# Attention denominators: inverses taken one key-tile pair earlier, spread by two transfers of 64 rows instead of one of 128

## The reference, cut to what matters

```python
scores = jnp.einsum('bhsr,bhlr->bhsl', q_r, k_r)       # 16 heads, 100 rows, 1444 keys
attn = jax.nn.softmax(scores, axis=-1)
ctx_c = jnp.einsum('bhsl,bld->bhsd', attn, kv_r)       # 64 values per head and row
ctx_lat = jnp.einsum('bhsd,hkd->bhsk', ctx_c, w_kc_kv)
return ctx @ Wo.T
```

## Time and profile before

| what | value |
|---|---|
| runs | 3496.22, 3482.72, 4833.27 us; median 3496.22 |
| profiled execution | 3511.37 us, span 3509.6 us |
| mean granted TensorE clock in it | 0.911 |
| latent attention (groups and heads) | about 964.8 to 3255 us of the span |
| one group in steady state | 290.5 us (1265.2 to 1555.7 us) |
| busy in that group: PE, DVE, POOL, ACT | 256.66, 213.18, 169.33, 137.54 us |

### The profile page before, as it was taken

One profiled execution on the slowest core, in us unless ns is written; L12 is line 12 of the kernel. 1 busy time (PEld: TensorE's weight loads), 2 busy tenths in 40 slices (PEclk: granted clock), 3 DMA queues, 4 the chain that ended last, 5 costly groups with the idle time before them and its releaser, 6 DMA issues. The chain is left out here.

```text
span 3509.6 us, 61563 instructions
## 1 busy us (share of the span) xinstructions
PE 2942.7 (84%) x18344; PEld 1971.0 (56%) x18352; DVE 2449.7 (70%) x4170; ACT 1488.0 (42%) x3074; POOL 1640.1 (47%) x1196
## 2 busy tenths in 40 slices
PE   6999979999788998998898898889889889887244
PEld 4777779998544554554454455555446455444123
DVE  5877754444576786687677677668777767775787
ACT  1323322222254454445435435444443553544456
POOL 0000022222465565555556565556565656564567
PEclk9888879999899998999999999899999999998566
DMA  4000010002101000100101000110010100010100
GB/s 105 0 0 0 0 50 5 9 9 51 29 13 19 20 13 15 22 13 15 19 14 21 14 20 16 16 21 16 14 21 11 19 16 16 10 45 13 60 13 24
DMA packets 128325, 71.04 MB, mean 20 GB/s; under 512 B 81663, under 2 KB 122591, under 8 KB 127961
## 3 DMA queue, kind: packets, MB, share of 16 engines
q1 hardware_dynamic: 128024, 67.44, 8.6%
HBM read 56.95 MB, written 10.04 MB: 19 GB/s over the span
## 5 line engine op out<-in xcount | busy, mean ns | idle before, releaser
L1178 POOL TENSOR_TENSOR c_psum<-c_p 120x800 f32<-120x800 f32 (+1 forms) x384 | 745.5, 1945 | 737.0 <-ACT c_p L1462 339.9
L1462 ACT ACTIVATE c_p<-c_s_ps 120x400 f32<-120x400 f32 (+1 forms) x1536 | 659.2, 507 | 497.0 <-PE c_s_ps L1623 439.6
L1256 DVE TENSOR_REDUCE c_mpart<-c_m_ps 128x1 f32<-128x484 f32 x1080 | 656.5, 651 | 164.5 <-PE c_m_ps L1530 159.9
L1635 PE MATMUL c_o_ps<-c_p,c_val 120*64 120x400 f32 (+1 forms) x3072 | 629.2, 533 | 27.5 <-ACT c_onum L1429 16.3
L1530 PE MATMUL c_m_ps<-c_kmax,c_q 64*128 64x484 f32 x1080 | 340.8, 471 | 174.1 <-DVE c_mpart L1256 170.3
L1530 PEld LDWEIGHTS c_m_ps<-c_kmax,c_q 64*128 64x128 f32 x1080 | 153.2, 194 | 405.8 <-DVE c_mpart L1256 329.4
L1283 DVE TENSOR_TENSOR c_acc<-c_acc,c_psum 120x800 f32<-120x800 f32 x256 | 322.4, 1259 | 63.8 <-POOL c_psum L1178 61.8
L1635 PEld LDWEIGHTS c_o_ps<-c_p,c_val 120*64 120x64 f32 (+1 forms) x3072 | 194.4, 141 | 292.4 <-issue 170.1
L1169 POOL TENSOR_TENSOR l_rr<-c_psum,l_rr 96x400 f32<-96x400 f32 x256 | 260.8, 1039 | 208.0 <-DVE l_rr L1305 207.9
L1566 PE MATMUL c_s_ps<-c_xt,l_a 128*96 128x400 f32 x1536 | 309.6, 352 | 23.4 <-DVE l_rr L1305 21.5
L1619 PE MATMUL c_s_ps<-c_q,c_k 64*120 64x400 f32 (+1 forms) x1536 | 319.8, 375 | 2.3 <-ACT c_p L1462 2.3
(11 more groups left out here) (251 smaller groups left out, 5075.3 us busy)
## 6 DMA issues: line engine op xcount, KB each, us to landing
c_rdb<-l_denominators SPq DMA_DIRECT2D x64, 200.0 KB
c_kv<-in_ctx SPq DMA_DIRECT2D x32, 360.0 KB
c_mrow<-c_mneg SPq DMA_DIRECT2D x288, 0.5 KB, 2.0
x_rows<-in_x SPq DMA_DIRECT2D x4, 800.0 KB
x_spill<-x_rows SPq DMA_DIRECT2D x8, 400.0 KB
l_xa<-x_spill SPq DMA_DIRECT2D x8, 400.0 KB
c_xr<-x_spill SPq DMA_DIRECT2D x32, 100.0 KB
x_spill<-c_xr SPq DMA_DIRECT2D x32, 100.0 KB
```

The source lines that it names most:

```text
L1178: g.tensor_tensor(psum[0:k, u % 2, :], p[0:k, 2 * u % 4, :], p[0:k, (2 * u + 1) % 4, :], ALU.add).then_inc(psum_ready, 1)
L1256: v.tensor_reduce(mpart[:, t, bank:bank + 1], m_ps[:, bank, 0:4 * KP], AX.X, ALU.max, negate=True).then_inc(mpart_ready, 1)
L1462: a.activation(p[0:k, w % 4, i * HALFQ:(i + 1) * HALFQ], s_ps[0:k, (2 * w + i) % 4, 0:HALFQ], ACT.Exp).then_inc(exp_ready, 1)
L1635: mm = pe.matmul(o_ps[i * DL:(i + 1) * DL, 0:HALFQ], val[0:k, j % 2, r, :], p[0:k, w % 4, i * HALFQ:(i + 1) * HALFQ], start=(r == 0), stop ...
```

## The change

Three edits, all in `phase_l1_attention`. DVE's `invert` stands after pair q = 2 instead of q = 3 (slots 5 and 17 instead of 7 and 19). The spread is two transfers of 64 partitions each, which count 32 on the semaphore together. In SP's list the write of the inverses goes ahead of `load_combined(it, j, 6)` (first half) or of `load_combined(it, j + 1, 2)` (second half), and the spread goes ahead of `load_combined(it, j + 1, 3)`. In the heads the order stays, and only the two transfers are new. The fold stays where it was, behind `load_combined(it, j, 5)` or `(it, j + 1, 1)`.

```diff
@@ spread_inverses
                     sp.wait_ge(ct_ready, PRIMED + ch)
-                    sp.dma_start(rdb[:], io["den"].rearrange("(i n) -> i n", i=2).unsqueeze(1).broadcast_to((2, DL, HALFQ))).then_inc(rdb_loaded, 16)
+                    for i in range(2):
+                        sp.dma_start(rdb[i * DL:(i + 1) * DL, :], io["den"][i * HALFQ:(i + 1) * HALFQ].partition_broadcast(DL)).then_inc(rdb_loaded, 16)
@@ SP, group, first half
                         if j > 0:
                             fold_denominators(b * CH - 1)
+                        if j > 0:
+                            write_inverses(b * CH - 1)
                         load_combined(it, j, 6)
                         if j > 0:
-                            write_inverses(b * CH - 1)
                             spread_inverses(b * CH - 1)
@@ SP, group, second half
                             load_combined(it, j + 1, 0)
                             load_combined(it, j + 1, 1)
                         fold_denominators(b * CH)
+                        write_inverses(b * CH)
                         if j + 1 < G:
                             load_combined(it, j + 1, 2)
+                        spread_inverses(b * CH)
+                        if j + 1 < G:
                             load_combined(it, j + 1, 3)
-                        write_inverses(b * CH)
-                        spread_inverses(b * CH)
@@ DVE, normalise
-                    v.wait_ge(rdb_loaded, 16 * (ch + 1))
+                    v.wait_ge(rdb_loaded, 32 * (ch + 1))
@@ DVE, group
-                        if (j, c) != (0, 0) and q == 3:
+                        if (j, c) != (0, 0) and q == 2:
                             invert(ch - 1)
```

## The result

The changed kernel takes 3389.89 us (median of 4 runs, 3388.19 to 3399.07); the kernel before took 3499.6 us beside it. Ratio 0.9707, 95% interval 0.9666 to 0.9749: faster by 2.9%. In a second series it had 3402.29 us and 0.9753 (0.9708 to 0.9799). The profiled execution took 3399.07 us against 3511.37, so 112.3 us less, where 75 were forecast. The ratio compares fast runs alone, so the run of 4833.27 us of the kernel before is not in it. Faster by over 2% had been given 0.46, within 2% 0.51.

A forecast was written before the change was run, and what follows sets the result against it. Bound by PE and DVE waiting for each other, with 153.3 us of DVE waits for the spread: (17.2 - 8.3) x 8 = 71 plus 4 gives 75 us off 3511.4, 3436, or 3421 on the median's scale; range 3375 to 3475.

The forecast's parts named there:

- What bounds the kernel, and the narrow transfer: DVE waits 153.3 us for the spread inverses, whose transfer runs on about two of 16 DMA engines, 7.3 us to use.
- All waits at the normalising go: At DVE's L1268, all 18.2 us of waiting per group for the spread inverses would go.
- What that is worth: Gain from the removed waits at L1268: 17.2 us per group, bounds 9.3 and 22.
- The first, second and fourth place: Three of a group's eight waits at L1268, with PE standing still behind: on the path, 13.6 us with the slow clock.
- The other five: The group's remaining waits at L1268, without a PE gap behind: 8.0 us of DVE's time, worth 3.6.
- The inverse two slots earlier: New DVE waits for the fold at L1264, 6.6 us per group; with one slow stretch of clock a loss of 8.3.
- The one more slow stretch: Behind the new waits at L1264, PE's clock at its lower level once more per group, costing 1.7 us.
- The end: The last L1268 waits 5.65 us; the shorter landing takes 4.7 off, 0.7 already counted: 4 us gained.
- the waits are traded: Rival: DVE's time returns only where PE stands still, against 8.3 us new per group; 26 us gained, 3470; chance 0.29.
- the slower case: Rival: the fold wait at L1264 costs more than the spread wait it replaces; 15 us slower, 3511; chance 0.07.
- The case of more coming back: Rival: new waits fall into DVE's later ones, clock stays 1.00: 134 us gained, 3363, in part 3390; chance 0.11.

The follow-up runs named there:

- the inverse back: The changed kernel with DVE's inverse moved back behind pair q = 3, all else as changed: 3356.57 us, ratio 0.9615; a second time 3349.53 us, 0.9596.
- the fold ahead: The changed kernel with the fold issued ahead of load_combined(it, 1, 5) and of load_combined(it, j + 1, 1) for j = 0 and 1: 3366.27 us, ratio 0.9626.
- The dose: The changed kernel with the inverse behind q = 3, plus an unread 128x128 DVE copy ahead of each of a group's 40 accumulator additions: 3420.04 us, ratio 0.9797.
- the kernel with both edits: The changed kernel with the inverse behind q = 3 and the fold ahead of the row transfers: 3347.56 us, ratio 0.9586; a second time 3341.19 us, 0.9562.

## Why the prediction was right, and where its sizes were off

*What bounds the kernel, and the narrow transfer:* right, and now shown. With the order of before, 64 rows outermost take the wait from 153.3 to 18.6 us; in the changed order two transfers of the old shape leave 39.0 us, where one leaves 37.2. From the first issue to the use 2.6 us were taken; it is 3.4. It did no harm in the groups, where the spread had time to spare.

*All waits at the normalising go:* right, 1.8 us are left, at the end.

*What that is worth, 17.2 us per group:* 18.7 with the inverse back, where 0.6 us of waiting is left. The sum hid two errors of opposite sign, and that it came out so near is luck. The first, second and fourth place were put at 13.6 us. Made wide alone they give 290.1 - 281.2 = 8.9 us, and with the wait that this leaves in the first place (273.3 - 271.4) 10.8. I had added 4.0 us of clock on top of PE's gaps; which part of the 13.6 was too large the runs don't say. The other five were put at 3.6 of 8.0 us, because PE shows no gap behind them; they gave 7.9 for the 9.3 us of waiting that went per group, so some 7 for 8.0. The step that failed was to read "no gap of PE behind the wait" as "not on the path". DVE's next longer pause does not take the wait up: it comes 5.1 us after the fifth place and lasts 2.2 us, in all of the six groups, both in the kernel before and in the one with the two wide transfers alone.

*The inverse two slots earlier:* the three places and their waits came out as worked (3.8, 1.75 and 1.6 forecast; 3.79, 0.99 and 1.62 measured; some 57 us forecast, 51.7 measured). Their price was put at 8.3 us per group and measured at 5.7. The one more slow stretch did come, 3.4 us at the lower level behind PE's gap of 3.42 us in every group; it was put at half of 3.4. What was too high is the sum of the two terms, 6.6 of waiting and 1.7 of clock: taking the waits away by the fold ahead gave back only 4.0 us per group. Moving the inverse back after that gave 2.3 to 2.6 more, without any wait, and for this the prediction had no term. In the kernel with the fold ahead the clock is at its lower level for 12.5 us per group instead of 5.7, so the 4.0 us are net of that; why the slow stretches moved so stays open. This item is the larger part of the error, 2.6 of 4.1 us per group; the other 1.5 is in the item before.

*The end:* 4 us forecast, 3.9 measured, in part by luck. The wait was to fall by 4.7 us, of which 0.7 had been counted with the groups; it fell by 3.9, because the pair takes 3.4 us to use and not 2.6.

*The rivals:* that the waits are traded is refuted, as is the slower case. The case of more coming back (3363 to 3390, chance 0.11) is where the time landed, at its edge. Both of its reasons held in part. Most slow stretches went with PE's gaps, though the clock did not stay at 1.00 behind the new waits. And these cost less than their length, 4.0 us for 6.5 by the fold ahead, where this case had 3.

From the kernel before (158.1 us of waits, 290.1 us per group) to the one with the inverse back (6.5 us, 271.4) it is 18.7 us for 19.0 of waiting. The dose shows 0.72 per us for DVE's time, and single steps lie between 0.6 (the fold ahead) and 1.2 (the first, second and fourth place, 8.9 us for 7.5). The clock rose with it from 0.95 to 0.98, and PE's busy time fell from 1527.12 to 1482.98 us in six groups for the same matmuls. I varied neither by itself, so what share is theirs is not shown. The clock alone does not order the kernels: the changed one has the higher clock, 0.99, and is slower by 5.7 us per group than the one with the inverse back at 0.98.

## What to carry to other kernels

Before a wait for a transfer is hidden by moving things, look at how wide the transfer runs: here the one with 2 outermost kept the DMA engines 11% busy for 5.7 us, and the same bytes with 64 outermost kept them 29% busy for under 2. When a step is moved earlier, ask for its inputs too; here the fold that feeds it stayed behind other transfers in one queue, and a third of the gain (5.7 of 18.7 us per group) was given back with this move. And a wait on the second-busiest engine can cost most of its length, here 0.8 us per us, also where the busiest engine shows no gap right behind it: look whether the waiting engine's later pauses can take it up.

## What the runs showed of the hardware

The kernel with the fold ahead has no waits at either place and still takes 273.1 us per group, 2.3 and 2.6 more than the two runs with the inverse back as well (270.8 and 270.5). DVE is busy 1302.95 us in six groups there and 1295.35 in the better kernel, with the same instructions. The difference lies in an operation with two SBUF inputs, `c_k<-c_kd,c_k`: its 72 instructions are busy 71.4 us against 60.6. The third batch of one group, in the kernel with the fold ahead, DVE's and POOL's timelines:

```profile
1950.31 2.31 DVE L1255 TENSOR_TENSOR c_k<-c_kd,c_k 64x484 fp32r<-64x484 f32 x1
...
1950.22 1.88 POOL L1187 TENSOR_TENSOR c_psum<-c_p 120x800 f32<-120x800 f32 x1 [1.83 <-ACT c_p L1471]
```

and in the kernel with both edits:

```profile
1946.32 0.64 DVE L1255 TENSOR_TENSOR c_k<-c_kd,c_k 64x484 fp32r<-64x484 f32 x1
...
1946.34 2.38 POOL L1187 TENSOR_TENSOR c_psum<-c_p 120x800 f32<-120x800 f32 x1 [1.93 <-ACT c_p L1471]
```

Where POOL is 0.09 us ahead, DVE's operation takes 2.31 us, until 0.5 us after POOL's end; where DVE is 0.02 us ahead, it takes 0.64 and POOL 2.38 instead of 1.88. In the kernel before, the reductions from PSUM hardly vary and the additions of two SBUF inputs do:

```profile
L1256 DVE TENSOR_REDUCE c_mpart<-c_m_ps x1080: 639/651/665, 977.3 to 3192.4; 128x1 f32<-128x484 f32 x180
...
L1283 DVE TENSOR_TENSOR c_acc<-c_acc,c_psum x256: 930/992/2729, 988.5 to 3225.8; 120x800 f32<-120x800 f32 x128
```

(min/median/max in ns). The Trainium skill states this in "SBUF — State Buffer", section "SBUF: two separate sides": DVE and GpSimd share a pair of ports under an exclusive lock, a DVE operation with two SBUF inputs takes part in it against a GpSimd operation that reads SBUF, and who comes second is blocked for the whole instruction of the first. These rows agree. That this is why the earlier inverse costs DVE 1.3 us per group beside its waits is argued from them; no kernel here kept the two engines apart.

The same shows at the normalising, which also has two SBUF inputs, and it is where most of DVE's extra busy time went. In six groups the 48 of them are busy 27.6 us in the kernel before, and 42.5 us with the inverse back, 15 of the 20.5 us that DVE is busy more there. In the seventh place DVE had waited 3.3 us for the spread and then took 0.58; now it starts without a wait, and takes 2.27 us in the mean, in the third group with POOL's `c_psum<-c_p` under way from 0.20 us before its start to 0.44 us before its end. So a part of the wait that was removed came back as a longer operation.
